# Storing finished units by four indexed row transfers instead of one strided transfer

## The reference

```python
A = relu((adj + adj.T) * 0.5);  d = rowsum(A) ** -0.5
x = x + relu((I - d A d) @ (layernorm(x) @ W))          # per batch, 2048 x 2048 by 2048 x 128
t = layernorm(x)                                        # tokens, 128 features
p = softmax(t @ router_w.T);  w, e = top2(p);  w = w / sum(w)
y = t
for i in range(8):
    y = y + combine(w, e)[:, i] * (gelu(t @ w1[i] + b1[i]) @ w2[i] + b2[i])
out = x + y
```

## Time and profile before

| | |
|---|---|
| time, 3 runs | 965.71 us median (964.76 to 966.42) |
| profiled execution | 967.4 us, of which the span from first to last instruction is 965.7 us |
| granted TensorE clock, mean | 0.976 |
| busy | PE 900.4 us (93%), DVE 645.8 (67%), ACT 517.5 (54%), POOL 310.2 (32%) |

### The profile page before, as it was taken

One profiled execution on the slowest core, in us unless ns is written; L12 is line 12 of the kernel. 1 busy time (PEld: TensorE's weight loads), 2 busy tenths in 40 slices (PEclk: granted clock), 3 DMA queues, 4 the chain that ended last, 5 costly groups with the idle time before them and its releaser, 6 DMA issues.

```text
span 965.7 us, 15348 instructions
## 1 busy us (share of the span) xinstructions
PE 900.4 (93%) x4446; PEld 728.1 (75%) x4446; DVE 645.8 (67%) x1558; ACT 517.5 (54%) x899; POOL 310.2 (32%) x312
## 2 busy tenths in 40 slices
PE   4776799999999999999999688999999999999996
PEld 4774588888787888878888566777777777777774
DVE  3987543657877533333424376888888888888886
ACT  3665233243444312122121366888888888888885
POOL 0699234564666544463444400000000000000000
PEclk9997899999999999999999779999999999999999
DMA  9983265585766247866666653777777777777771
GB/s 285 330 239 119 98 240 218 210 293 170 251 219 203 81 158 265 299 254 237 252 233 250 245 194 141 265 265 265 265 265 265 265 265 265 264 264 266 265 265 44
DMA packets 93022, 222.98 MB, mean 231 GB/s; under 512 B 8856, under 2 KB 59568, under 8 KB 81072
## 3 DMA queue, kind: packets, MB, share of 16 engines
q1 hardware_dynamic: 86752, 211.59, 62.2%
q0 software_dynamic: 2560, 8.39, 2.2%
q10 hardware_dynamic: 3664, 2.43, 0.9%
HBM read 157.89 MB, written 64.49 MB: 230 GB/s over the span
## 4 chain that ended last, share of the span: by engine, by line
PE 82%; DVE 6%; POOL 4%; issue 3%; ACT 2%; DMA 2%; DVEq 0%; ACTq 0%; SPq 0%; POOLq 0%
PE bank L906 11%; PE bank L908 11%; PE bank L907 11%; PE bank L1272 7%; PE bank L1259 6%; PE bank L1261 6%; PE bank L1260 6%; PE bank L1274 6%; PE bank L1273 6%; POOL col_sum L543 2%; PE bank L854 2%; PE bank L330 2%; DVE y_lo L699 2%; PE bank L862 2%; PE bank L1280 2%
## 5 line engine op out<-in xcount | busy, mean ns | idle before, releaser
L1348 DVE TENSOR_TENSOR gated<-c_all,act_h 128x512 f32<-128x512 f32 x256 | 177.0, 692 | 63.6 <-ACT act_h L1310 58.5
L1310 ACT ACTIVATE act_h<-bank,b_sb 128x512 f32<-128x512 f32 x256 | 176.6, 690 | 77.8 <-PE bank L1261 74.9
L1353 DVE TENSOR_TENSOR g_lo<-gated,g_hi 128x512 fp32r<-128x512 f32 x256 | 175.5, 685 | 0.1
L1317 ACT ACTIVATE g_hi<-gated 128x512 fp32r<-128x512 f32 x256 | 159.0, 621 | 1.7 <-DVE gated L1348 1.7
L1244 POOL DMA_DIRECT2D out<-fin x32 | 24.3, 761 | 387.2 <-DVE fin L1361 382.1
L906 PE MATMUL bank<-y_hi,stage 128*128 128x512 f32 x256 | 111.7, 436 | 3.7 <-DVE y_lo L699 3.6
L1272 PE MATMUL bank<-g_hi,w_hi 128*128 128x512 f32 x256 | 107.8, 421 | 3.7 <-DVE g_lo L1353 3.6
L1259 PE MATMUL bank<-z_e,w_hi 128*128 128x512 f32 x256 | 105.3, 411 | 5.6 <-DMA z_e<-z_scratch 5.6
L988 POOL TENSOR_TENSOR rstd<-var_eps,neg_half 128x4 f32<-128x4 f32 x32 | 48.5, 1516 | 180.4 <-DVE var_eps L1025 179.9
L906 PE MATMUL bank<-y,stage 128*128 128x512 f32 x256 | 104.5, 408 | 0.0
L993 POOL TENSOR_SCALAR z<-x,mv,rstd 128x128 f32<-128x128 f32 x128 | 101.4, 805 | 3.4
(11 more groups left out here) (118 smaller groups left out, 1588.6 us busy)
## 6 DMA issues: line engine op xcount, KB each, us to landing
c_all<-c_scratch SPq DMA_DIRECT2D x64, 1024.0 KB, 8.0
s_scratch<-stage SPq DMA_DIRECT2D x14, 2048.0 KB, 8.4
stage<-s_scratch SPq DMA_DIRECT2D x14, 2048.0 KB, 8.0
z_e<-z_scratch SPq DMA_DIRECT2D x32, 512.0 KB, 6.9
z_scratch<-z_hl SPq DMA_DIRECT2D x31, 512.0 KB, 2.7
x_raw<-in_x SPq DMA_DIRECT2D x32, 256.0 KB, 7.4
x_res<-in_x SPq DMA_DIRECT2D x32, 256.0 KB, 7.3
r_e<-res_scratch SPq DMA_DIRECT2D x32, 256.0 KB, 2.7
```

What stands on the lines that cost most here:

```text
L1310: act.activation(v.act_h[e % R][:, :], ps_h[e % 2][:, :], ACT.Gelu, bias=v.b1_sb[:, e:e + 1]).then_inc(gelu_done, 1)
L1317: act.activation(v.g_hi[e % R][:, :], v.gated[e % R][:, :], ACT.Copy).then_inc(hi_done, 1)
L1348: dve.tensor_tensor(out=v.gated[e % R][:, :], in0=v.c_all[s][:, e, :], in1=v.act_h[e % R][:, :], op=ALU.mult).then_inc(gated_done, 1)
L1353: dve.tensor_tensor(out=v.g_lo[e % R][:, :], in0=v.gated[e % R][:, :], in1=v.g_hi[e % R][:, :].bitcast(FP32), op=ALU.subtract).then_inc(lo ...
```

## The change

Three edits are made. A table `row_of` of 128 row numbers per partition is made once on POOL in setup with an `iota`, ahead of the wait before the `affine_select` that finishes `ident`. The table's column `u * 4 + q` holds on partition `p` the output row of unit `u`, batch `q`. The single store of a unit becomes four indexed transfers, each of 128 rows of 512 bytes (64 KB), with the row numbers read from that column. And POOL's loop over the units is written out, 32 times four transfers, while the other engines keep theirs. Each store now adds 64 to its semaphore, so DVE's wait becomes `32 * u - 32 * s`, and the last waits become `16 * Q * (U // 2)`.

```diff
+        v.row_of = sb("row_of", [P, 2, MB, Q], mybir.dt.int32)
...
+        pool.iota(v.row_of[:, :, :, :], pattern=[[Q * N, 2], [P, MB], [N, Q]], base=0,
+                  channel_multiplier=1).then_inc(v.rows_made, 1)
         pool.wait_ge(consts_made, 5 + E)
         pool.affine_select(out=ident[:, :], in_=ident[:, :], compare_op=ALU.not_equal, fill=1.0,
...
-        def store(h, s, u):
-
+        out_rows = v.out.rearrange("b n f -> (b n) f")
+
+        def store(u):
+            s = u % 2
             pool.wait_ge(fin_done, u + 1)
-            half, n = (0, u) if isinstance(u, int) else (u // MB, u & (MB - 1))
-            rows = v.out_units[bass.ds(half, 1), bass.ds(n, 1)]
-            pool.dma_start(rows.rearrange("a c p q f -> p (a c q) f"),
-                           v.fin[s][:, :].rearrange("p (q f) -> p q f", f=P)).then_inc(stored[s], 16)
-
-        over_units(pool, store)
+            for q in range(Q):
+                pool.indirect_dma_start(out_rows, bass.IndirectOffsetOnAxis(ap=rows[:, u * Q + q:u * Q + q + 1], axis=0),
+                                        v.fin[s][:, q * P:(q + 1) * P], None).then_inc(stored[s], 16)
+
+        pool.wait_ge(v.rows_made, 1)
+        rows = v.row_of[:, :, :, :].rearrange("p h n q -> p (h n q)")
+        for u in range(U):
+            store(u)
         for s in range(2):
-            pool.wait_ge(stored[s], 16 * (U // 2))
+            pool.wait_ge(stored[s], 16 * Q * (U // 2))
...
-            wait(dve, stored[s], 8 * u - 8 * s)
+            wait(dve, stored[s], 8 * Q * u - 8 * Q * s)
```

More of the change, by code:

```diff
@@ L451, in setup_stage @@
 def setup_stage(nc, sem, v):
-    E, MB, CW, Q = v.E, v.MB, v.CW, v.Q
+    E, MB, CW, Q, N = v.E, v.MB, v.CW, v.Q, v.N
     low, up, s_tri, ident = v.low, v.up, v.s_tri, v.ident
@@ L463, in setup_stage @@
     zeroed = sem("zeroed")
+    v.rows_made = sem("rows_made")
     deg_step = v.deg_step = sem("deg_step")
```

## The result

| | before | changed |
|---|---|---|
| time, median of 20 runs each | 966.06 us (962.93 to 969.51) | 968.78 us (965.98 to 972.06) |
| ratio, 95% interval | | 1.0029 (1.0018 to 1.0041) |
| a second time, on another chip | 966.80 us, 23 runs | 968.68 us, 12 runs: 1.0023 (1.0010 to 1.0037) |
| span of the profiled execution | 965.7 us | 970.3 us |

The changed kernel is slower by about 2.7 us, 0.29%. That is more than the 0.2% that I had set as the bound of what can be told. So it is slower, where I had forecast 1.3 us and no difference that can be told. The time lies inside the range. The two spans differ by more than the medians, 4.6 us: the profiled execution of the changed kernel, 972.06 us, was the slowest of its 20. Of the 4.6 us, 3.3 lie behind the last `finish`.

The account below looks back on a forecast made before the run. PE, busy 93% of the span, was taken to set the pace, with all costs hidden except in the last unit: 4d - 2.7 = +1.3 us at d = 1.0, on 965.71 giving 967.0 us; range 965.0 to 971.4 us.

Parts of the forecast that it names:

- The covers: Setup and steady units: iota, DVE's register instruction and waits, SP's loads and POOL's four issues are hidden, cost 0.
- The rival that GpSimd's longer work slows DVE: Every unit: some five DVE operations behind `finish` grow; 48 ns each gives +7 us, 974 us; chance 0.07.
- The last landing: Last unit: the last transfer lands 1.4 + d after its issue, 2.4 us at d = 1.0.
- the sum 4d - 2.7: Last unit, `finish` to landing: 1.73 + 4d against 4.4 us, a change of +1.3 us at d = 1.0.
- d: Price of one indexed issue on POOL, taken as 1.0 us, bounded between 0.19 and 2.94 us.
- three issues in a row: Last unit: three of four serial issues delay the last transfer by d each, with d taken as 1.0 us.
- spaced wider than they last: Sign against the prediction: POOL's issue starts lie further apart than the forecast spacing of about 1.0 us, their own length.
- The start behind `finish`: Last unit: the first of the four issues starts 0.33 us after the last `finish`, instead of 1.68.
- the closing part: Program end: about 0.7 us more of closing waits behind the last landing, up to 965.7 us.
- the indexed issue is dear: Rival, last unit: d above 1.16 us, slower; 969.0 us at 1.5, 974.8 at 2.94; chance 0.34.
- its point of 1.16: The d in us above which the last unit's change, 4d - 2.7, passes the 1.93 us that can be told.
- The 1.35 us of saving: Last unit: writing the loop out cuts `finish` to store from 1.68 to 0.33 us; otherwise 0.5 to 0.6 us saved.

Follow-up runs that it names:

- e2: Changed kernel with only the last unit's store made a single plain transfer: 965.09 us, 0.9995 of the kernel before.
- e3: Kernel before with GpSimd's loop written out and only the last unit stored by four indexed transfers: 969.03 us, 1.0035 of before.
- e4: Changed kernel with four plain 64 KB transfers per unit in place of the indexed ones: 965.78 us, 1.0006 of the kernel before.
- e8: Changed kernel with the last unit stored by SP in one plain transfer: 961.98 us, 0.9949 of the kernel before.
- e5: Kernel before with GpSimd's loop written out and the last unit's single plain store issued by SP: 963.01 us, 0.9955; again 963.28 us, 0.9969.
- e1: Kernel before with only GpSimd's loop over units written out, stores left single and plain: 965.40 us, 0.9996 of before.

## Why the prediction came out as it did

**What held.** The place: no loss is shown but that of the last unit. e2 removes the loss by changing four transfers of 128, e3 brings it back with four. The covers held too: the iota (0.38 us, PE starts with the load as before), DVE's register instruction (e4, stage 339.7 us), the waits on `stored`, the loads of SP (8.3 us to landing for `c_all` and 6.6 for `z_e` in the median, where it was 8.0 and 6.9), and GpSimd's four issues per unit. The rival that GpSimd's longer work slows DVE has happened, but small: 21 to 44 of the 256 `g_lo` operations last some 0.05 us longer in the four traces with indexed issues in the stage, at most two in a unit and not five, and none in the eight traces without. PE's wait for `g_lo` stays at 0.3 us per unit, and e8 is no slower than e5. So the prediction's cost of 0 came out in the time, and its products at 0.69 us only in the median. The last landing was put at 2.4 us behind its issue and took 2.3.

**What failed is the size of the sum 4d - 2.7 at d = 1.0.** Four of its terms were off, all but one in the same direction.

- The price of three issues in a row. I took 1.0 us each from the duration of the first plain issue. The duration was right, 0.96, but the starts are 1.26 us apart, since 0.30 us lie between two indexed issues. That is 3.79 instead of 3.0: +0.8 us. The prediction named "spaced wider than they last" as a sign against it, and the issue row of plain stores could not show it, as there was never a second one behind a first. e4 shows that plain ones have no such gap.
- The start behind `finish`, 0.57 us instead of 0.33: +0.24. GpSimd was taken to be free when the last `finish` ended. The last two `finish` are 5.1 us apart and not 12.1, and four issues with their start fill 5.4. The 5.1 us could have been read off in the kernel before. With starts 1.26 us apart the four would just have fitted (0.28 + 3 x 1.26 + 0.96 = 5.0); the first two of them lasted 1.15 and 1.08 us.
- The drain, +1.1 us, was in no term. I had counted the closing part as a constant 0.7 us. It depends on the number of transfers, and e4 has the same 1.38 us with plain ones.
- The last issue to the end of the wait was 0.1 us shorter than put.

Together 0.8 + 0.24 + 1.1 - 0.1 = 2.0 us, which makes +1.3 into the +3.3 of the trace; the timed difference is 2.7 (1.7 to 4.0 by the interval). The rival "the indexed issue is dear" had the right outcome, and its mechanism at the right place: 1.26 us from start to start is above its point of 1.16, though the issue itself, 0.96, is not. Without the drain the trace's end would be 2.2 us longer than before, just above the bound of 1.93.

That the time lies in the range is in part luck. The range reached up to 971.4 for a dearer issue; the drain, a third of what was added to the end, was in no term and in no rival.

**The 1.35 us of saving** were partly right for a reason that I could not see: e1 shows that writing the loop out is worth 0.58 us at the end. The further 0.8 us of the late store do not come back in the changed kernel, because its crossing falls in unit 28, where it is hidden. The same fact makes its drain long, as 15 transfers stand from there on. So the 1.68 us became 0.57: 0.58 and 0.8 us less, and 0.27 more since the issues of the unit before were still running.

**Left open.** The stage is 339.5 to 339.9 us long in some traces and 340.4 to 340.5 in others. I could not tie this to any edit. Both traces of the changed kernel have the longer one, so a share of the change in it is not excluded; it moves the profiled span by up to 1 us and is within the scatter of the timing. Why 0.30 us lie between two indexed issues is also not shown by any row. In the stage single issues last 1.15 and 1.50 us, and at the end, where DVE rests, 0.95 to 0.96; where DVE works, some `g_lo` operations last longer too. What the two engines share was not tried.

## What to carry to other kernels

Here a store that another unit follows cost GpSimd six times its work and was free; price such a change where nothing follows it, with the spacing of issues and not their duration, and with the closing drain. If stores go through GpSimd, give the last one to an idle SP queue: it took 1.75 us off the end here (e1 to e5), in the indexed kernel 5.4. Before you believe a gap in front of one single transfer, count which number it has in its queue.

## What the runs showed of the hardware that was not expected

- An indexed transfer of 128 rows of 512 bytes occupies GpSimd for 0.96 us, and the next starts 0.30 us later. A plain one of the same 64 KB takes 0.54 us with no gap, one of 256 KB 0.75 us.
- GpSimd's drain at the end grows by 0.08 us for each transfer from that place on: 0.24 us for 1, 0.32 for 2, 0.49 for 4, 1.05 for 11, 1.14 for 12, 1.38 for 15, and 2.61 for all 31 where none crossed. It is the same for plain and indexed transfers.
- While indexed issues run, 21 to 44 of the 256 `g_lo` operations of DVE last 0.70 to 0.745 us and not 0.69. Beside plain issues none does.
- A store of 256 KB issued by SP started 0.03 us behind `finish` and was over 2.4 us behind it; issued by GpSimd it took 3.0 us at best.
